# Scans of two pairs of heads back to back in every second step, the second into the bank where x is turned

## The reference

```python
proj = xn @ in_proj_w.T                      # gate, x|B|C, dt: 8192 + (8192 + 1024 + 1024) + 128 columns
xBC  = silu(causal_conv4(xBC) + conv_b)      # one filter of 4 taps per channel
dt   = clip(softplus(dt + dt_bias), 0.001, 100)
# 128 heads of 64 channels in 8 groups; 16 heads share B and C; chunks of 128 tokens
cs   = cumsum(dt * A);  L = exp(cs_l - cs_s) for s <= l
y    = ((C B^T) * L) (x * dt)  +  contribution of the chunk before  +  D * x
yg   = y * silu(gate)
out  = yg * rsqrt(mean(yg^2 over the 1024 channels of a group) + eps) * norm_w
s    = out @ out_proj_w.T                    # 8192 -> 512
f    = 16 experts (56 wide), the best 2 weighted: (silu(xn g^T) * (xn u^T)) d^T
```

## Time and profile before

| | |
|---|---|
| time, median of 3 (lowest, highest) | 1638.48 us (1638.3, 1638.57) |
| the profiled execution: its time, its span | 1638.45 us, 1636.3 us |
| granted clock of PE | 0.997 of full speed |
| products of a block of 128 channels (L449 to L451 into `pj`) | 3624 instructions, 479.3 + 472.4 + 472.6 us |
| scan (L661, L665) | 2048 instructions, 160.5 + 99.4 us busy |
| `x_turn` (L650) | 512 instructions, 76.6 us busy |
| exponents to `decay` | 128 DMAs of 768 KB |

### The profile page before, as it was taken

One profiled execution on the slowest core, in us unless ns is written; L12 is line 12 of the kernel. 1 busy time (PEld: TensorE's weight loads), 2 busy tenths in 40 slices (PEclk: granted clock), 3 DMA queues, 4 the chain that ended last, 5 costly groups with the idle time before them and its releaser, 6 DMA issues.

```text
span 1636.3 us, 28479 instructions
## 1 busy us (share of the span) xinstructions
PE 1598.9 (98%) x8484; PEld 1269.6 (78%) x8484; DVE 1411.6 (86%) x1664; ACT 1198.4 (73%) x2305; POOL 957.9 (59%) x593
## 2 busy tenths in 40 slices
PE   7899989999999999999999999999999999999998
PEld 5677867877778777787777777877778778778776
DVE  6553699988998899998898899989898899889987
ACT  3432688778787778878787878778787878778782
POOL 4522266666566556666566656665576655666563
PEclk9999999999999999999999999999999999999999
DMA  4322344434343344433443334443343434334432
GB/s 150 94 98 94 115 143 149 148 106 150 131 145 135 122 148 147 143 112 123 151 156 128 119 131 152 140 131 129 138 158 110 137 130 158 134 114 148 155 129 90
DMA packets 83719, 216.48 MB, mean 132 GB/s; under 512 B 10576, under 2 KB 12880, under 8 KB 83424
## 3 DMA queue, kind: packets, MB, share of 16 engines
q1 hardware_dynamic: 83264, 214.15, 38.9%
q10 hardware_dynamic: 288, 0.30, 0.1%
HBM read 209.43 MB, written 4.98 MB: 131 GB/s over the span
## 4 chain that ended last, share of the span: by engine, by line
PE 84%; DVE 8%; issue 3%; ACT 3%; POOL 1%; DMA 0%; ACTq 0%; DVEq 0%; POOLq 0%; SPq 0%
PE pj L449 15%; PE pj L451 14%; PE pj L450 14%; PE pr L449 8%; PE pr L450 7%; PE pr L451 7%; PE sc L661 7%; PE sc L665 3%; PE tb L650 3%; DVE conv L1309 2%; POOL w_lo L1014 1%; DVE wo_lo L1373 1%; ACT decay L915 1%; PE pr L639 1%; DVE xc L1323 1%
## 5 line engine op out<-in xcount | busy, mean ns | idle before, releaser
L1014 POOL TENSOR_TENSOR w_lo<-stg,w_hi 128x512 fp32r<-128x512 f32 x316 | 496.2, 1571 | 348.7 <-ACT w_hi L889 263.8
L449 PE MATMUL pj<-xT_hi,w_hi 128*128 128x512 f32 x1208 | 479.3, 397 | 15.8 <-POOL w_lo L1014 7.2
L451 PE MATMUL pj<-xT_hi,w_lo 128*128 128x512 f32 x1208 | 472.6, 391 | 0.0
L450 PE MATMUL pj<-xT_lo,w_hi 128*128 128x512 f32 x1208 | 472.4, 391 | 0.0
L1309 DVE SCALAR_TENSOR_TENSOR conv<-pj,par,conv 128x510 f32<-128x510 f32 (+2 forms) x480 | 357.7, 745 | 80.5 <-ACT conv L897 67.1
L915 ACT ACTIVATE decay<-decay,dtg 128x256 f32<-128x256 f32 (+1 forms) x1024 | 379.0, 442 | 0.0
L1048 POOL TENSOR_TENSOR xc<-xc,thg 128x512 f32<-128x512 f32 x128 | 203.1, 1587 | 188.1 <-DVE xc L1360 188.0
L1054 POOL TENSOR_TENSOR sqsum<-sqsum,sq 128x512 f32<-128x512 f32 x112 | 218.1, 1947 | 114.5 <-ACT sq L941 111.0
L449 PEld LDWEIGHTS pj<-xT_hi,w_hi 128*128 128x128 f32 x1208 | 227.8, 189 | 73.2 <-issue 14.2
L451 PEld LDWEIGHTS pj<-xT_hi,w_lo 128*128 128x128 f32 x1208 | 227.9, 189 | 48.5
L450 PEld LDWEIGHTS pj<-xT_lo,w_hi 128*128 128x128 f32 x1208 | 228.1, 189 | 45.4
(11 more groups left out here) (178 smaller groups left out, 1995.0 us busy)
## 6 DMA issues: line engine op xcount, KB each, us to landing
stg<-wstream SPq DMA_DIRECT2D x387, 256.0 KB, 2.7
decay<-cs_scr SPq DMA_DIRECT2D x128, 768.0 KB, 4.3
acc<-hid SPq DMA_DIRECT2D x8, 256.0 KB, 4.8
out<-acc SPq DMA_DIRECT2D x8, 256.0 KB, 2.0
dt_scr<-decay SPq DMA_DIRECT2D x1, 1024.0 KB, 4.9
gate_scr<-part SPq DMA_DIRECT2D x4, 256.0 KB, 2.0
dtg<-dt_scr SPq DMA_DIRECT2D x16, 64.0 KB, 4.2
stg<-hid SPq DMA_DIRECT2D x4, 256.0 KB, 4.9
```

Of the source, the lines that this page charges most:

```text
L449: nc.tensor.matmul(dst, hi_w, hi_x, start=first, stop=False)
L450: nc.tensor.matmul(dst, hi_w, lo_x, start=False, stop=False)
L451: return nc.tensor.matmul(dst, lo_w, hi_x, start=False, stop=last)
L1014: nc.gpsimd.tensor_tensor(w_dest(n, 1), stg[:, s % RING, :], f32(w_dest(n, 0)), ALU.subtract).then_inc(S["wl"], 1)
```

## The change

The scan of an odd pair goes to the bank `tb` instead of `sc`, and the two scans of an even and an odd pair follow each other in the odd step. In an even step PE turns x of pair s+1 where it did; in an odd step it does so as its last action. What waits, and what is done by twos, follows from that:

```diff
+        yb = [sc, tb]
             def x_turn(g, half, j):
                 pe.wait_ge(S["silu"], at(g, half, NX, j + 3))
                 pe.wait_ge(S["ms"], at(g, half, 1, 0 if j >= 2 else -1))
                 pe.wait_ge(S["xdt"], at(g, half, NJ, j))
+                if j % 2 == 0:
+                    pe.wait_ge(S["u"], at(g, half, NJ, j))
...
             def scan(g, half, j):
-                pe.wait_ge(S["u"], at(g, half, NJ, j))
+                pe.wait_ge(S["u"], at(g, half, NJ, j - 1))
+                if j == 1:
+                    pe.wait_ge(S["ms"], at(g, half, 1, 0))
...
-                        nc.tensor.matmul(sc[hd, c0:c0 + 2 * P], xdt[:, j % 2, 2 * b, hd],
+                        nc.tensor.matmul(yb[j % 2][hd, c0:c0 + 2 * P], xdt[:, j % 2, 2 * b, hd],
...
 # PE, step
-                if has_pair(g, half, s + 1):
+                if s % 2 == 0 and has_pair(g, half, s + 1):
                     x_turn(*pair(g, half, s + 1))
-                if has_pair(g, half, s):
+                if s % 2 == 1 and has_pair(g, half, s):
+                    scan(g, half, s - 1)
                     scan(g, half, s)
                 if len(mine) > 1:
                     channel_block(g, half, mine[1])
                 if with_out:
                     out_of_step(g, half, s)
+                if s % 2 == 1 and has_pair(g, half, s + 1):
+                    x_turn(*pair(g, half, s + 1))
 # ACT, step
+                before = (g, 0) if half == 1 else (g - 1, 1)
                 if s == 0 and with_out:
+                    done = [(*before, NJ - 2), (*before, NJ - 1)]
+                elif s >= 2 and s % 2 == 0 and has_pair(g, half, s - 1):
+                    done = [(g, half, s - 2), (g, half, s - 1)]
+                else:
+                    done = []
+                if done:
+                    y_hi(*done[0])
+                    square(*done[0])
+                    y_hi(*done[1])
                 if has_pair(g, half, s + 2):
                     drops(*pair(g, half, s + 2), 1)
...
                     decays(*pair(g, half, s + 2))
+                if done:
+                    square(*done[1])
 # POOL, step
                 if with_out and s == 0:
-                    add_square(*before, NJ - 1)
+                    add_square(*before, NJ - 2)
...
-                if s >= 2 and has_pair(g, half, s):
-                    add_square(g, half, s - 1)
+                if s >= 4 and s % 2 == 0 and has_pair(g, half, s):
+                    add_square(g, half, s - 2)
                 for i in range(1, n):
                     split_low(g, half, s, i)
-                if has_pair(g, half, s):
+                if with_out and s == 0:
+                    add_square(*before, NJ - 1)
+                if s >= 2 and s % 2 == 0 and has_pair(g, half, s):
+                    add_square(g, half, s - 1)
+                if s % 2 == 1 and has_pair(g, half, s):
+                    gated(g, half, s - 1)
                     gated(g, half, s)
 # DVE, add_scan
-                                               in1=sc[:, :], op0=ALU.mult, op1=ALU.add).then_inc(S["u"], 1)
+                                               in1=yb[j % 2][:, :], op0=ALU.mult, op1=ALU.add).then_inc(S["u"], 1)
 # DVE, step
-                if has_pair(g, half, s + 1):
+                if s % 2 == 0 and has_pair(g, half, s + 1):
                     x_times_dt(*pair(g, half, s + 1))
-                if has_pair(g, half, s):
+                if s % 2 == 1 and has_pair(g, half, s):
+                    add_scan(g, half, s - 1)
                     add_scan(g, half, s)
                 for m in mine[1:]:
                     taps(g, half, m)
-                if s >= 1 and has_pair(g, half, s - 1):
+                if s >= 2 and s % 2 == 0 and has_pair(g, half, s - 1):
+                    y_lo(g, half, s - 2)
                     y_lo(g, half, s - 1)
...
                 for m in mine[1:]:
                     x_silu(*of_half(g, half, m), m)
+                if s % 2 == 1 and has_pair(g, half, s + 1):
+                    x_times_dt(*pair(g, half, s + 1))
```

More of the change, by code:

```diff
@@ L664, in scan @@
                         hd = slice(h * HD, (h + 1) * HD)
-                        mm = nc.tensor.matmul(sc[hd, c0 + P:c0 + 2 * P], xdt[:, j % 2, 2 * b + 1, hd],
+                        mm = nc.tensor.matmul(yb[j % 2][hd, c0 + P:c0 + 2 * P], xdt[:, j % 2, 2 * b + 1, hd],
                                               decay[:, j % NDEC, 2 * h + b, 2 * P:3 * P], start=False, stop=True)
@@ L955, in step @@
                     drops(*pair(g, half, s + 2), 0)
-                if s >= 1 and has_pair(g, half, s - 1):
-                    y_hi(g, half, s - 1)
-                    square(g, half, s - 1)
+                before = (g, 0) if half == 1 else (g - 1, 1)
                 if s == 0 and with_out:
-                    before = (g, 0) if half == 1 else (g - 1, 1)
-                    y_hi(*before, NJ - 1)
-                    square(*before, NJ - 1)
+                    done = [(*before, NJ - 2), (*before, NJ - 1)]
[7 more added lines that the diff above has]
+                    y_hi(*done[1])
                 if has_pair(g, half, s + 2):
@@ L997, in _ @@
                 step(G - 1, 1, s)
-            y_hi(G - 1, 1, NJ - 1)
-            square(G - 1, 1, NJ - 1)
+            for j in (NJ - 2, NJ - 1):
+                y_hi(G - 1, 1, j)
+                square(G - 1, 1, j)
         @block.gpsimd
@@ L1086, in _ @@
                 step(G - 1, 1, s)
+            add_square(G - 1, 1, NJ - 2)
             add_square(G - 1, 1, NJ - 1)
@@ L1412, in step @@
                     taps(g, half, m)
-                if s >= 1 and has_pair(g, half, s - 1):
+                if s >= 2 and s % 2 == 0 and has_pair(g, half, s - 1):
+                    y_lo(g, half, s - 2)
                     y_lo(g, half, s - 1)
                 if s == 0 and with_out:
+                    y_lo(*before, NJ - 2)
                     y_lo(*before, NJ - 1)
@@ L1468, in _ @@
             finish(3)
+            y_lo(G - 1, 1, NJ - 2)
+            finish(4)
             y_lo(G - 1, 1, NJ - 1)
-            finish(4)
             finish(5)
```

## The result

The changed kernel takes 1688.0 us (1686.19 to 1688.91), the kernel before 1638.53 beside it: ratio 1.0301 [1.0283, 1.0319], 49 us slower. Forecast were 20 us slower, at most 42. The sign is right, more than half of the size was missed. Profiled were 1686.19 us, span 1684.1.

A forecast was written before the change was run, and what follows sets the result against it. PE, busy in 98% of the span, was taken to bound the kernel. From 1638.45 us, minus 18 gain, plus 33 for six busy halves and 4.6 for the two end groups, came 1658; range 1643 to 1680.

The forecast's parts named there:

- PE's gain: Turns and scans on PE: two steps cost 3.93 us instead of 4.22, saving 18 us over 64 pairs of steps.
- The turn's wait in busy halves: Halves with output-projection blocks prepared on DVE: turns ending steps 3, 5, 7 wait for `add_scan`, 5.5 us per half.
- Step 7: End of a busy half's step 7: `add_scan` done at E + 8.01, turn due at E + 5.69, wait 2.3 us.
- E: The moment at which a step's first block of x ends on PE; the forecast counts DVE's and PE's times from it.
- In the light half ... no wait: Halves where only step 0 prepares an output-projection block: `add_scan` done at E + 5.1, turn due at E + 5.69.
- step 3 of the busy half: Turn's wait taken as 1.4 us: E some 1.6 us nearer step 2's, one more `y_hi` on ACT, 0.62 or less.
- The edits by twos: Reordered `add_scan` and `y_lo` on DVE, `y_hi` and `square` by twos on ACT: no cost beyond the turn's waits.
- The two ends: First and last group of heads: new waits of 2.3 us each, the lower bound.
- The fourth: Rival: weights and exponents late by up to 0.5 us in 64 odd steps, column sums late; about 1675, chance 0.21.
- The second: Rival: DVE catches up in even steps with one POOL meeting less, only step 7 waits; 1638, chance 0.07.
- the third: Rival: `add_scan` is done when the turn is due, so the 18 us gain stands alone; 1620, chance 0.09.
- the signs of being wrong that I set: Turn doesn't wait, light half does, a block of x waits for its weights, or ACT waits for exponents.

The follow-up runs named there:

- e7: Changed kernel with both pairs' turns in the even step, B/C products behind the scans, two weight pieces ahead of even-pair exponents: 1623.39 us, ratio 0.9897.
- e3: Changed kernel with the B and C products behind the two scans and `mask_products` behind `add_scan`: 1671.86 us, ratio 1.020.
- e6: Changed kernel with the edits of e3 and e5 together: 1668.64 us, ratio 1.0171.
- e5: Changed kernel with SP issuing two weight pieces of the next step ahead of the even pair's exponents: 1681.32 us, ratio 1.0257.
- e4: Kernel before, with SP's exponents of even pairs waiting for one scan more than they must: 1657.68 us, ratio 1.0121.
- e10: e7 with the low parts of y one residual addition sooner at the end of the program: 1620.34 us, ratio 0.9884.
- e2: Changed kernel with even pairs' exponents issued by ACT at the end of its odd step instead of by SP: 1853.2 us, ratio 1.1312.

## Why the prediction was right and wrong

**PE's gain: right.** Forecast were 0.29 us per pair of steps. The scan pair cost 2.98 where 2.97 was worked out, so the second scan is at the lower bound (1.30), not at the upper. With the waits of turns and B/C products away, the light stretch of e7 is 88.7 against 89.9, 1.2 us for four pairs of steps, 0.30 each (e7 has moved the turns as well, so this isn't the scans alone). In the changed kernel the sum of the lateness less the growth of the stretches leaves 18 us for 56 pairs, 0.32 each.

**The turn's wait in busy halves: right in place, too large in size.** It stands where it was put, three times. In the half shown the turns came late by 1.06, 1.36 and 1.37, 3.8 us together instead of 5.5; over seven halves 28 instead of the 35 in my sum. Step 7 was most off. DVE there:

```profile
654.68 2.30 DVE L1332 SCALAR_TENSOR_TENSOR conv<-pj,par,conv 128x510 f32<-128x510 f32 x3
...
657.56 0.74 DVE L1383 SCALAR_TENSOR_TENSOR xc<-xc,par,tb 128x512 f32<-128x512 f32 x1
```

Its taps were forecast to end at E + 6.61 and end at 656.98 = E + 5.61; from there to the end of the second `add_scan` are 1.32 us, 1.4 forecast. So the term that I mis-sized is DVE's lateness in step 7. I had carried it over from the kernel before. PE's waits in steps 3 and 5 give DVE time to catch up. That fits e3, where the wait of the B/C products is gone and step 7 waits 1.8 us instead of 1.2, but no run tests it by itself.

**"In the light half ... no wait": wrong, the step that failed.** Forecast were 1.1 us less for each light half, measured 1.8 more, a difference of 2.9 in each of seven stretches. Of the 28 us that the forecast missed between the profiled executions this is 20; the two ends add 13, and the busy stretches, at +3.2 instead of some +3.9 on average, give 5 back. The turns of steps 3 and 7 came late by 1.4 us per light half, the B/C products by 1.3. Three things are behind it:
- DVE's start. I let the taps of a light half end at E + 3.73, as in the kernel before, so that `add_scan` was done at E + 5.1 against 5.69. In the half shown they end at E + 4.95 in step 3 and E + 5.21 in step 7, and the second `add_scan` another 1.3 us later. Late weights are the smaller part: in e6, where they are on time, the same taps still end at E + 4.62 and E + 4.87, and the turns still wait (its step 2 and step 3, where E is 0.09 ahead of the scan's start):

```profile
497.11 2.31 DVE L1337 SCALAR_TENSOR_TENSOR conv<-pj,par,conv 128x510 f32<-128x510 f32 x3 [1.04 <-ACT conv L912]
...
504.35 0.65 PE L673 MATMUL sc<-decay,xdt 128*64 128x256 f32 x4
506.58 2.30 DVE L1337 SCALAR_TENSOR_TENSOR conv<-pj,par,conv 128x510 f32<-128x510 f32 x3
...
510.33 0.63 PE L660 MATMUL tb<-cst,xc 128*128 128x128 f32 x4 [0.22 <-DVE xc L1388]
```

  The rest, 0.9 to 1.1 us, is of the kind that I had put into step 3 of the busy half and not here: E comes nearer to that of the step before, and ACT has one more `y_hi` ahead of the tap. DVE's two `y_lo` come with it, below. How it divides among these no run shows.
- SP. I named that weights queue behind the exponents' wait, gave it 0 to 0.5 us per odd step and took 0, because the exponents themselves would arrive in time. The bound was wrong: the queue is held until the even scan ends, and then two exponent loads of 768 KB and four pieces go out in one burst (490.42 to 494.5 us). A piece lands in 4.1 us (page after), 2.7 before. ACT waited 2.87 us in the step shown. With the rest of the change in place that is worth 7 us (e5), 0.6 in each light half; put alone into the kernel before it costs 19 (e4).
- The B/C products. I counted their 1.31 us on PE, but not that the scan that leaves step 4 pulls them nearer to their input: 1.3 us of lateness in a light half, 0.6 in the busy one at 625.59. No term and no rival had it. e3 gives 16 us, 1.6 in each light half.

**The edits by twos: not free.** In step 2 of the light half the two `y_lo` take 3.17 us; in e7's last half two took 1.28 (at 1589.45 us). POOL works beside the slow ones:

```profile
504.55 1.29 POOL L1071 TENSOR_TENSOR sqsum<-sqsum,sq 128x512 f32<-128x512 f32 x1 [0.60 <-ACT sq L951]
505.79 1.74 POOL L1031 TENSOR_TENSOR w_lo<-stg,w_hi 128x512 fp32r<-128x512 f32 x1
```

On the whole DVE won as much: `y_lo` went from 863 to 1340 ns, `x_silu` from 1542 to 1124, all of DVE from 1411.6 to 1387.0 us. That the meetings with POOL become fewer fits. But one of them now stands ahead of the turn of step 3. The port pair locked for an instruction, which the prediction cites from the Trainium skill ("SBUF — State Buffer", "Terms"), agrees with both durations: the slow pair ends at 508.08, 0.55 us behind the end of POOL's addition and low part, and beside the fast one POOL stands still from 1589.48 to 1590.22. But a meeting doesn't always cost DVE. Beside the `x_silu` of 0.68 us at 995.13, which the prediction took for one without a meeting, POOL had a low part from 995.12 on, and it was POOL that was slow, with 1.84 us instead of 1.30.

**The two ends: 12.8 us instead of none.** By my terms, what lies ahead of the first column sums and behind the last would have come out even (2.3 of wait against 2.3 of gain); measured are +6.3 and +6.5. In the first group two turns waited 3.4 and 5.0 us, where DVE already kept PE waiting before the change. At the end the product of the last but one pair waited 3.7 us for `y_lo`, which now comes a step later and stood behind four residual instructions. I had taken 2.3 us for each, the lower bound, since in the first group a new wait would partly replace an old one. It did: PE's waits for DVE at the blocks fell from 7.3 to 1.7 us there. But the turns brought 9.8. And the waits of 5.0 and 3.7 us drew a second price (last section).

**The rivals.** The fourth (1675, chance 0.21) named SP's queue and was nearest, in part by luck. It priced late weights at 16 us where e5 finds 7. Its late column sums show once, with 0.5 us of wait. What made up the difference, the B/C products and DVE in light halves, it didn't name. The second and the third are out: the turn waits in steps 3 and 5 as well. The range ended 5 us above the fourth case, and the time lies 8 us beyond it. Of the signs of being wrong that I set, the wait in a light half came true. ACT waited for weights, not for exponents, and no block of x on PE waited for its weights between 294 and 1548 us.

## What to carry to other kernels

When an instruction is moved later, look up who waits for it on the queue that issues DMAs, and price everything behind that wait in the queue; issue what needs no such wait first. When an effect of the change is priced in one kind of step (here: a step that begins sooner, and one operation more ahead of it), price it in every kind, even where slack seems to cover it. And when several waits stand in one loop, taking one away at a time can measure too little, here 51 us instead of 65: try them together before the idea is given up.

## What the runs showed of the hardware

- After some waits PE's products start 0.43 us apart for seven to thirteen instructions instead of 0.23. The changed kernel, first group; the granted clock is 0.50 from 233 to 237 us, which is the lower of its two levels (1.2 GHz):

```profile
233.31 1.08 PE L655 MATMUL tb<-cst,xc 128*128 128x128 f32 x4 [5.04 <-DVE xc L1383]
...
235.05 0.63 PE L453 MATMUL pj<-xT_hi,w_lo 128*128 128x512 f32 x1
235.47 0.63 PE L451 MATMUL pj<-xT_hi,w_hi 128*128 128x512 f32 x1
...
238.40 0.40 PE L452 MATMUL pj<-xT_lo,w_hi 128*128 128x512 f32 x1
238.63 0.40 PE L453 MATMUL pj<-xT_hi,w_lo 128*128 128x512 f32 x1
```

  It happened behind waits of 5.0, 3.7 (at 1664 us) and 3.4 us (e7), and not behind another of 3.4 at 212.61 nor behind the changed kernel's waits of 1.9 and less. But in other runs it happened behind 2.0 us (e10 at 222.73), 1.9 (e6 at 1201.20) and 1.15 (e7 at 1180.95), so the length of the last wait doesn't tell it. The slow products cost about 1.8 us at 233 us and 2.6 at 1603 in e7.
- Weights landed later where SP issued them in a burst with exponents: 4.1 us in the median (changed kernel), 4.4 in e4, against 2.7 before and in e5, with the same bytes.
- A load of 768 KB issued by ACT landed in 5.6 us, one by SP in 4.7, in the same run (e2). They were issued at other moments of a step, so that the queue makes the difference isn't shown.
